# Two-layer vision block on one core: image 0's convolution chain inside the dense expert layer, gate logits from unnormalised rows, first expert tiles inside image 1's chain

## What is computed

```python
x = x + _L0_conv_ref(_ln_c(x), ...)
t = _to_tokens(x)
t = t + _L0_ffn_ref(_ln_t(t), ...)          # 8 experts, all computed
x = _from_tokens(t, x)
x = x + _L1_conv_ref(_ln_c(x), ...)
t = _to_tokens(x)
t = t + _L1_ffn_ref(_ln_t(t), ...)          # 16 experts, top 2 of a softmax

def _L1_conv_ref(x, ...):
    h = _group_norm(1x1 conv to 32 channels)
    z = relu(_group_norm(9-tap column conv + 9x9 depthwise conv of h))
    z = relu(_group_norm(1x1 conv to 128 channels))
    return z + x

def _L1_ffn_ref(x, ...):
    probs = softmax(x @ gate_w + gate_b); two largest, scaled to sum 1
    hidden = silu(x @ w1[e]) * (x @ w2[e])
    return sum over the two e of gate * (hidden @ w3[e])
```

## Time and profile before

| | us |
|---|---|
| median of 3 runs (721.44 to 726.18) | 723.17 |
| the profiled execution | 719.29 |
| its span, first to last instruction | 717.5 |
| busy: TensorE, GpSimd, VectorE, ScalarE | 599.5, 424.2, 358.2, 356.0 |
| mean granted TensorE clock, share of full | 0.902 |

### The profile page before, as it was taken

One profiled execution on the slowest core, in us unless ns is written; L12 is line 12 of the kernel. 1 busy time (PEld: TensorE's weight loads), 2 busy tenths in 40 slices (PEclk: granted clock), 3 DMA queues, 4 the chain that ended last, 5 costly groups with the idle time before them and its releaser, 6 DMA issues.

```text
span 717.5 us, 16640 instructions
## 1 busy us (share of the span) xinstructions
PE 599.5 (84%) x5672; PEld 506.2 (71%) x5673; DVE 358.2 (50%) x1040; ACT 356.0 (50%) x843; POOL 424.2 (59%) x484
## 2 busy tenths in 40 slices
PE   2677788879699999999999989887869999999900
PEld 2566677667377776677777667676869999999900
DVE  6977788655600612030014554573755555555533
ACT  4466678975564445751135532224036665666600
POOL 1667799764785686663342200077567777777771
PEclk9989999988888899999997998886879999999965
DMA  9452222211256353231490000011223332333536
GB/s 308 142 139 79 80 69 83 58 52 50 86 201 221 115 201 132 90 132 45 138 320 18 1 0 1 0 49 53 64 58 99 109 97 83 109 99 93 199 117 212
DMA packets 59042, 75.35 MB, mean 105 GB/s; under 512 B 9470, under 2 KB 49366, under 8 KB 58302
## 3 DMA queue, kind: packets, MB, share of 16 engines
q1 hardware_dynamic: 51614, 60.49, 26.7%
q0 software_dynamic: 5632, 11.62, 4.8%
q10 hardware_dynamic: 1728, 2.36, 0.9%
HBM read 57.96 MB, written 23.81 MB: 114 GB/s over the span
## 4 chain that ended last, share of the span: by engine, by line
PE 62%; DVE 10%; POOL 10%; issue 7%; ACT 7%; DMA 3%; SPq 1%; DVEq 0%; POOLq 0%; ACTq 0%
PE bank L800 13%; PE bank L762 9%; PE bank L866 8%; PE bank L745 8%; PE bank L811 6%; PE bank L831 4%; PE bank L722 3%; POOL gathered_or_att L570 3%; POOL padded_or_w L561 3%; PE bank L316 3%; POOL returned L640 2%; POOL gathered_or_att L579 2%; ACT normed L911 2%; PE bank L881 2%; PE bank L791 2%
## 5 line engine op out<-in xcount | busy, mean ns | idle before, releaser
L605 POOL TENSOR_TENSOR padded_or_w<-padded_or_w,gathered_or_att 128x384 f32<-128x384 f32 x96 | 95.3, 999 | 76.9 <-ACT padded_or_w L985 73.1
L621 POOL DMA_INDIRECT sorted_x<-normed,slot x72 | 71.7, 995 | 97.0 <-DVE slot L1328 75.8
L640 POOL DMA_INDIRECT returned<-gathered_or_att,home_of_slot x104 | 102.7, 987 | 31.7 <-issue 22.3
L985 ACT ACTIVATE padded_or_w<-bank,moe_b 128x384 f32<-128x384 f32 x96 | 55.4, 580 | 102.9 <-PE bank L745 102.8
L762 PEld LDWEIGHTS bank<-moe_or_conv,padded_or_w 128*128 128x128 f32 x576 | 82.3, 201 | 32.0 <-issue 10.9
L762 PE MATMUL bank<-moe_or_conv,padded_or_w 128*128 128x128 f32 x576 | 85.6, 288 | 0.0
L745 PE MATMUL bank<-chan_major,moe_or_conv 128*128 128x384 f32 x192 | 83.0, 520 | 0.0
L660 PE MATMUL bank<-padded_or_w 64*64 64x64 f32 x1152 | 49.3, 239 | 26.7 <-issue 15.3
L660 PEld LDWEIGHTS bank<-padded_or_w 64*64 64x64 f32 x1152 | 43.2, 150 | 36.4 <-issue 36.4
L1357 DVE TENSOR_TENSOR att_or_moe<-att_or_moe,bank 128x256 f32<-128x256 f32 x104 | 43.7, 420 | 50.3 <-PE bank L811 27.0
L999 ACT ACTIVATE att_or_moe<-bank 128x256 f32<-128x256 f32 x104 | 40.0, 384 | 55.9 <-PE bank L800 55.9
(11 more groups left out here) (181 smaller groups left out, 1166.8 us busy)
## 6 DMA issues: line engine op xcount, KB each, us to landing
gathered_or_att<-combine SPq DMA_DIRECT2D x24, 768.0 KB, 4.1
padded_or_w<-windows SPq DMA_DIRECT2D x192, 48.0 KB, 1.9
...
```

The source lines that it names most:

```text
L605: nc.gpsimd.tensor_tensor(HB[n % DRING], HB[n % DRING], GB_[k % 3][:, n % 4, :], ALU.mult).then_inc(S("gated"), 1)
L621: nc.gpsimd.indirect_dma_start(xs_dram[b], bass.IndirectOffsetOnAxis(ap=POS[b][:, k, t:t + 1], axis=0), TNR[b][:, t, :], None).then_inc(S( ...
L640: nc.gpsimd.indirect_dma_start(yt_dram[b], bass.IndirectOffsetOnAxis(ap=HOMES[b][:, j:j + 1], axis=0), YR[k * RING + j % RING], None).then ...
L985: nc.scalar.activation(HB[n % DRING], banks[HBANK[n % 2]][:, 0:DG], ACT.Gelu, bias=B1C[:, e:e + 1]).then_inc(S("gelu"), 1)
```

## The change

Image 0's whole chain up to its slots and its scatter stands in the dense layer, closer packed: the taps six groups per step, the eight up-projections, the relu, the sum, the routing. The list behind the dense layer holds image 1's chain alone, with 20 of the 160 `KW` matmuls. The gate logits no longer wait for the last norm: the gate weights are centred once (`GC`), 18 matmuls take the rows of the first norm (`LB`, in two halves), 18 the convolution's output (`LZ`, three per group beside `XZ`), and VectorE adds both and scales by 1/std. So `RT` and `LG` of layer 1 are gone, and the normalised rows are needed by the scatter alone; ScalarE makes all of them. Square roots of three of the norms and of image 1's last two group norms become Newton steps on VectorE, those of image 0's group norms a power on GpSimd (`PG`). The table of tile experts is a phase of its own (`RJ`). The first 14 pipeline steps of image 0's tile loop (`MT`) stand between phases of image 1's chain, on all engines; the loop uses other PSUM banks, a tile's transpose and output share one, and ScalarE evicts the output before the silu.

```diff
...
+            (33, ("RX", 1)), (40, ("GC", 0)), *every(28, 4, groups("AN", "LR", 0, 1))])
...
-            (52, ("SQ", "XL", 0)), (52, ("LV", "XL", 0)), *every(53, 1, groups("LT", "XL", 0)), *every(54, 1, groups("XG", 0)),
-            *every(56, 2, groups("AN", "XL", 0)), (61, ("XC", 0)), (62, ("XCE", 0)), (62, ("GN", "XC", 0)), (65, ("GS", "XC", 0)), (67, ("GQ", "XC", 0)),
-            (69, ("XCH", 0)), *every(71, 1, taps(0, 0, 54)), (89, ("GN", "XM", 0)), (91, ("GS", "XM", 0)), (93, ("GQ", "XM", 0)), (95, ("XMH", 0)),
-            *every(96, 1, [("XU", 0, n) for n in range(4)])])
-        order += [("KW", 24, "gelu", DN), *normed("XL", 1), *[("XU", 0, n) for n in range(4, 8)], ("GN", "XU", 0), *groups("XG", 1), ("GS", "XU", 0), ("GQ", "XU", 0),
-                  ("XC", 1), ("XCE", 1), ("GN", "XC", 1), ("KW", 10, "hc_ready", 2 * NB), ("GS", "XC", 1), ("GQ", "XC", 1), ("XCH", 1), ("KW", 12, "hc_ready", 2 * NB), *groups("XUH", 0),
-                  *taps(1, 0, 9), *groups("XZ", 0), *groups("AN", "XL", 1), *taps(1, 9, 24), *routing(1, 0), *taps(1, 24, 54),
-                  *choice(1, 0, 1, 6), ("GN", "XM", 1), ("KW", 6, "hc_ready", 2 * NB), ("GS", "XM", 1), ("RP", 0), ("GQ", "XM", 1), ("XMH", 1), ("RS", 0),
-                  *[("XU", 1, n) for n in range(8)], ("GN", "XU", 1), ("KW", 30, "up_out", 8 * NB), ("GS", "XU", 1), ("GQ", "XU", 1), ("KW", 10, "up_out", 8 * NB), *groups("XUH", 1), *groups("XZ", 1),
-                  ("KW", 18, "up_out", 8 * NB), *routing(1, 1), ("KW", 34, "up_out", 8 * NB), *choice(1, 1, 1, 6), ("RP", 1), ("KW", 16, "up_out", 8 * NB), ("RS", 1),
-                  *[("M", b) for b in range(NB)], *[("F", b) for b in range(NB)]]
-
-        group_no = {ph: k for k, ph in enumerate(ph for ph in order if ph[0] in ("LNA", "YA", "RT", "LG", "RX", "XG", "XZ"))}
+            (52, ("LV", "XL", 0)), *every(52, .5, groups("LT", "XL", 0)), *every(53, .5, groups("XG", 0)),
+            *every(56, 2, groups("AN", "XL", 0)), (57, ("XC", 0)), (58, ("XCE", 0)), (58, ("GN", "XC", 0)), (59, ("LB", 0, 0)), (60, ("GS", "XC", 0)),
+            (61, ("LB", 0, 1)), (61, ("PG", "XC", 0)), (63, ("XCH", 0)), *every(64, 1 / 6, taps(0, 0, 54)), (66, ("GN", "XM", 0)), (68, ("GS", "XM", 0)),
+            (69, ("PG", "XM", 0)), (71, ("XMH", 0)), *every(72, 1 / 3, [("XU", 0, n) for n in range(8)]), (74, ("GN", "XU", 0)), (77, ("GS", "XU", 0)),
+            (78, ("PG", "XU", 0)), *every(79, .5, groups("XUH", 0)), *every(80, .25, [(kind, 0, g) for g in range(NG) for kind in ("XZ", "LZ")]),
+            (85, ("LN", "LR", 1, 0)), (85, ("LV", "LR", 1, 0)), (86, ("RC", 1, 0, 0)), (88, ("RE", 1, 0)), (89, ("RC", 1, 0, 1)), (90, ("RC", 1, 0, 2)),
+            (92, ("RC", 1, 0, 3)), *every(91, 2, groups("LT", "LR", 1, 0)[:2]), (94, ("RC", 1, 0, 4)), (95, ("RP", 0)), (96, ("PD", 1)), (96, ("RS", 0)),
+            *every(96, .5, groups("LT", "LR", 1, 0)[2:])])
+        order += [*normed("XL", 1), *groups("XG", 1), ("XC", 1), ("XCE", 1), ("GN", "XC", 1), ("LB", 1, 0), ("GS", "XC", 1), ("GQ", "XC", 1), ("XCH", 1),
+                  ("LB", 1, 1), *groups("AN", "XL", 1), ("RJ", 0), *taps(1, 0, 54),
+                  ("GN", "XM", 1), ("KW", 8, "hc_ready", 2 * NB), ("GS", "XM", 1), ("KW", 12, "hc_ready", 2 * NB), ("XMH", 1), *[("XU", 1, n) for n in range(8)],
+                  ("GN", "XU", 1), ("GS", "XU", 1), *tiles(0, 4), *groups("XUH", 1), *[(kind, 1, g) for g in range(NG) for kind in ("XZ", "LZ")],
+                  ("LN", "LR", 1, 1), *tiles(4, 6), ("LV", "LR", 1, 1), ("RC", 1, 1, 0), ("RE", 1, 1), *groups("LT", "LR", 1, 1), *tiles(6, 7), ("RC", 1, 1, 1),
+                  *tiles(7, 9), ("RC", 1, 1, 2), *tiles(9, 11), ("RC", 1, 1, 3), *tiles(11, 13), ("RC", 1, 1, 4), ("RP", 1), *tiles(13, 14), ("RS", 1), ("RJ", 1),
+                  *tiles(14, J + 4), ("M", 1), *[("F", b) for b in range(NB)]]
...
-            return ln[0] in ("LNA", "LR", "XL") and not (g % 2 == 0 and tuple(ln) in (("LNA", 0), ("LNA", 1), ("XL", 1), ("LR", 1, 0), ("LR", 1, 1)))
+            return ln[0] in ("LNA", "LR", "XL") and not (g % 2 == 0 and tuple(ln) in (("LNA", 0), ("LNA", 1), ("XL", 0), ("XL", 1)))
...
+        NEWTON = (("XL", 0), ("LR", 1, 0), ("LR", 1, 1))
...
-        UP = ((6, 7), (4, 5, 3, 2))
+        UP = ((6, 7), (4, 5))
...
+        HID_BANK, ROW_BANK = (6, 7), (2, 3)
...
+                    sp.wait_ge(S("y_used"), DN)
...
+                nc.gpsimd.tensor_tensor(gv[:, 9:10], gv[:, 5:6], EXPO[:, 0:1], ALU.pow).then_inc(S("gn_root"), 1)
...
+                ln_wait_all(pool, "LR", 1, b)
...
+            def norm_logits(b, h):
+                E, n = EX[1], group_no[("LB", b, 0)]
+                if h == 0:
+                    t_wait_read(pe, group_no[("GC", 0)])
+                    t_wait_all_read(pe, "XG", b)
+                    t_wait_bank(pe, n)
+                for t in range(h * TT // 2, (h + 1) * TT // 2):
+                    ins = nc.tensor.matmul(t_bank(n)[:, t * E:(t + 1) * E], QY[b][:, t * P:(t + 1) * P], GWC[:, :], start=True, stop=True)
+                if h:
+                    ins.then_inc(S("t_full"), 1)
+
+            def conv_logits(b, g):
+                E = EX[1]
+                pe.wait_ge(S("z3_ready"), b * NG + g + 1)
+                for t in range(g * TG, (g + 1) * TG):
+                    ins = nc.tensor.matmul(banks[LOGIT_BANK[b]][:, t * E:(t + 1) * E], QY[b][:, t * P:(t + 1) * P], GWC[:, :], start=True, stop=True)
+                if g == NG - 1:
+                    ins.then_inc(S("conv_logits"), 1)
...
-                    nc.tensor.transpose(banks[r % 2][:, 0:P], XS[h * RING + r], IDN).then_inc(S("x_transposed"), 1)
+                    if not isinstance(j, int) or j >= 6:
+                        pe.wait_ge(S("y_ready"), j - 5 + b * J)
+                    elif b and j < 2:
...
-                    if isinstance(j, int) and j == 0 and b == 0:
-                        pe.wait_ge(S("routed1"), 1)
                     pe.wait_ge(S("hid1"), j + 1 + b * J)
-                    if not isinstance(j, int) or b or j >= 2:
+                    if isinstance(j, int) and j + 4 >= J:
                         pe.wait_ge(S("y_ready"), j - 1 + b * J)
...
+                    if j >= 4:
+                        act.wait_ge(S("y_full1"), j - 3 + b * J)
...
                     if j < J:
                         xt(j, j % RING)
+                    if j >= 4:
+                        tail(j - 4, j % RING)
                     if 0 <= j - 2 < J:
                         nonlin(j - 2, (j - 2) % RING)
-                    if j >= 4:
-                        tail(j - 4, j % RING)
...
                 lv = ln_set(ph)
-                dve.wait_ge(S("ln_std"), lns.index(ph) + 1)
-                link(nc.vector.reciprocal(lv[:, 5, :], lv[:, 4, :]))
+                if ph in NEWTON:
+                    chain_done = lns.index(ph) + 1
+                    dve.wait_ge(S("ln_var"), chain_done)
+                    newton(lv[:, 3, :], lv[:, 5, :], lv[:, 4, :])
+                    link(ts(lv[:, 5, :], lv[:, 5, :], NEWTON_SCALE, None, ALU.mult))
+                else:
+                    dve.wait_ge(S("ln_std"), [ln for ln in lns if ln not in NEWTON].index(ph) + 1)
+                    link(nc.vector.reciprocal(lv[:, 5, :], lv[:, 4, :]))
                 nc.vector.scalar_tensor_tensor(lv[:, 6, :], lv[:, 0, :], -1.0, lv[:, 5, :], ALU.mult, ALU.mult).then_inc(S("ln_coef"), 1)
...
                 row, v, over_e, over_t = route_views(l)
 
                 if piece == 0:
+                    if l == 1:
+                        dve.wait_ge(S("conv_logits"), b + 1)
+                        link(tt(RT[:, 0, 0:c], LGP[b][:, :], banks[LOGIT_BANK[b]][:, 0:c], ALU.add))
+                        link(tt(row(0), row(0), over_e(ln_set(("LR", 1, b))[:, 5, :]), ALU.mult))
+                        link(tt(row(0), row(0), over_t(GB[:, :]), ALU.add))
...
+            def norm_logits(b, h):
+                if h == 0:
+                    return
+                E, m = EX[1], group_no[("LB", b, 0)]
+                lv = ln_set(("XL", b))
+                link(tt(ONE_STD[:, :], lv[:, 3, :], lv[:, 5, :], ALU.mult))
+                link(ts(ONE_STD[:, :], ONE_STD[:, :], 1.0, None, ALU.add))
+                t_wait_full(dve, m)
+                t_read(tt(LGP[b][:, :].rearrange("p (t e) -> p t e", e=E), t_bank(m)[:, 0:TT * E].rearrange("p (t e) -> p t e", e=E),
+                          ONE_STD[:, :].unsqueeze(2).broadcast_to([P, TT, E]), ALU.mult), m)
...
+            def newton(v, y, t):
+
+                link(ts(y.bitcast(i32), v.bitcast(i32), 1, None, ALU.logical_shift_right))
+                link(ts(y.bitcast(i32), y.bitcast(i32), -1.0, float(0x5f3759df), ALU.mult, ALU.add))
+                for three in (3.0, 12.0, 768.0):
+                    if v.shape[-1] == 1:
+                        link(nc.vector.scalar_tensor_tensor(t, y, y, v, ALU.mult, ALU.mult))
+                    else:
+                        link(tt(t, y, y, ALU.mult))
```

(16 more changed lines are left out.)

170 lines of the change are left out of this document (112 added, 58 removed).

## The result

Over 15 runs of each the changed kernel took 730.22 us (median, 724.36 to 742.86), the kernel before 721.62 (715.18 to 726.18). The ratio is 1.0111, 95% interval 1.0073 to 1.0149: slower by one per cent, as forecast (732 us, 1.2 per cent over 723.17). The profiled execution took 726.65 us, its span is 724.8 where 726.5 was forecast; before it was 717.5.

A forecast was written before the change was run, and what follows sets the result against it. GpSimd's indirect DMA queue behind image 1's slots was taken as the bound: 543.5 + 0.3 + 168.5 + 14.2 = 726.5 us span, 732 us on the scale of the median. Its own range was 728 to 740, the overall range 718 to 742.

The forecast's parts named there:

- What bounds: GpSimd's indirect DMA queue sets the end: image 1's slots, then 0.3 us, 130 DMAs in 168.5 and a 14.2 us tail.
- Stage 1: Dense layer, paced by TensorE: 16.2 us added, 8.0 old idle off, 6.0 stalls and 4.3 clock added; end at 406.7.
- The add behind the slots: On VectorE image 0's slots, 7.1 us, stand ahead of the dense layer's last add, which starts at 411.0.
- Stage 2: Image 1 from its norm to its exponentials, in five parts: 93.9 us instead of 115.5, 21.6 us shorter.
- Stage 3: Image 1 from exponentials to slots: 36.8 us instead of 16.2, 20.6 more, slots at 543.5.
- silence: After image 1's exponentials VectorE does nothing for 10.2 us, its multiply waiting for a silu queued on ScalarE.
- The signs named for a right forecast: GpSimd unbroken over 130 DMAs, first scatter 538 to 549, norm 408 to 417, VectorE silent some 10 us, clock 0.50.
- A: Rival, faster: clock holds at full speed, 16.1 us less, span 710.4, time 716; chance 0.14.
- B: Rival, no change: packed dense layer regains its idle time, stage 1 7.3 us shorter, time 725; chance 0.26.
- C: Rival, much slower: the tile loop becomes the bound, over 1.67 us a tile; time 744 at 1.8; chance 0.06.
- D: Rival: group norms' square roots on GpSimd are dear, holding the dense layer 7.8 us, time 740; chance 0.05.
- The Trainium skill's drain: Rule for ScalarE table switches: a drain of 1.38 us each, 2.66 instead of 1.28 for stage 3's silu load.

The follow-up runs named there:

- e3: Changed kernel with image 0's slots moved on VectorE behind image 1's first norm; 1.0109 of the time of the kernel before.
- e2: Changed kernel with ScalarE's 18 normalisations of image 1's rows moved behind tile step 13, tiles left in place; 1.0154 of the kernel before.
- e1: Changed kernel with image 0's tile steps 4 to 13 moved behind image 1's slots; no ratio, 4 executions of 717.48 to 733.17 us.
- e4: Changed kernel with all of image 0's tile steps, 0 to 13, moved behind image 1's slots; 0.9958 of the kernel before.
- e7: Changed kernel, all tiles behind image 1's slots, image 0's slots behind image 1's norm, GpSimd's additions before image 0's scatter, idle-filling matmuls added; 0.9874 of the kernel before.
- e8: Changed kernel with image 0's first 36 logit passes cut from two runs of 18 into six runs of 6; 1.0183 of the kernel before.

## Why the prediction was right, and which terms were off

**What bounds.** Right, term by term: slots to scatter 0.76 us (0.3 forecast), 130 DMAs 168.2 (168.5), tail 14.9 (14.2). Slots at 540.96 instead of 543.5, and 534.5 was break-even. In every run the span followed the slot time and the number of DMAs behind it, with up to 3 us between executions in the pace of the DMAs.

**Stage 1.** Dense layer finished at 405.1, forecast 406.7, and this agreement is in part luck. The matmul with which the output of image 1's first group begins stands at 281.33 in the profile of before and at 278.01 in this one. In the eleven kernels made by the change, alike up to there, it stands between 277.94 and 281.66, so I put these 3.3 us down to the execution and not to the change.

```profile
281.33 0.91 PE L760 MATMUL bank<-moe_b,att_or_moe 24*128 24x384 f32 x2
```

```profile
278.01 0.91 PE L844 MATMUL bank<-moe_b,att_or_moe 24*128 24x384 f32 x2
...
357.91 0.75 PE L970 MATMUL bank<-conv_mid,conv_w 32*128 32x288 f32 x4
...
369.46 0.74 PE L805 MATMUL bank<-gate_w_centred,qy 128*128 128x16 f32 x6
```

From that matmul to the end of the layer TensorE took 106.9 us before and 127.1 here, 20.2 more, where the terms of the forecast add up to 18.5; from there to the end of the span the profile lost 10.6 us and not 7.3, and the ratio of all executions, 1.0111, lies between (8.0 us). The terms were further off than their sum. The added work was some 4 us cheaper than 16.2: from start to start the 72 narrow passes took 7.4 us (10.0 forecast), four up-projections 1.4 (2.8). The rows that they were priced from lie at the half clock, the 4.75 us in part (0.57 from 228 to 230; that row is of layer 0, with 8 columns), the 5.57 us almost wholly (0.59 from 460 to 462, then 0.50), so part of the clock was charged twice. TensorE idled 3.2 us at the first norm, 2.1 at the up-projections, 1.1 at the relu and 2.6 at the exponentials, 9.3 us with the small ones, where 6.0 were charged. Of these, 5.2 had been for the first norm and its gelu; the 3.2 at the up-projections and the relu had been put at nothing; and the table swap, taken at 0.8, had left out the 1.61 us in which ScalarE waits for VectorE between its loads. The clock fell three times instead of once:

```profile
298.00:304.00 6.00, 6.00 (x26) 4.30 (x26) 0.73 (x4) 1.06 (x2) 2.13 (x3) 0.72 0.35 131
346.00:352.00 6.00, 4.54 (x23) 2.89 (x22) 3.08 (x7) 3.51 (x7) 2.92 (x3) 0.94 0.35 131
352.00:358.00 6.00, 5.41 (x24) 3.54 (x22) 1.48 (x3) 2.55 (x5) 0.99 (x1) 0.78 0.00 0
394.00:400.00 6.00, 6.00 (x29) 3.93 (x29) 5.76 (x12) 3.48 (x9) 3.56 (x4) 0.86 1.01 277
```

These falls cost some 5 us, against 4.3 charged: 6 us times what is missing to 1.00 in the four rows is 4.2, and 1.0 for the 2 us ahead of the last one, from 391.94. What is left of the 20.2 us puts the old idle and half-speed time at about 6.3 us, where 8.0 were taken off. The add behind the slots was right to 0.05 us (4.3 forecast, 4.35 measured in e3).

**Stage 2.** 94.9 us against 93.9: to the first tap 17.9 (18.2), taps 28.7 (28.7), to the first up-projection 9.1 (6.2), to the relu 18.0 (17.0), to the exponentials 21.3 (23.8). The miss in the third part is the operation that GpSimd's additions held for 3.3 us. The prediction had costed GpSimd by its own length and its cover, and had not asked what it does to VectorE beside it. The last part was 2.5 us shorter than forecast, which hides most of that miss.

**Stage 3.** 34.7 against 36.8, in the parts forecast: silence 9.2 (10.2), the choice and slots alone 16.7 (16.2), tiles and restarts 8.8 (10.5). e2 shows the cause of the silence, e1 and e4 the whole price. The signs named for a right forecast came, the clock at 0.50 beside the narrow matmuls only in part: in the dense layer all 72 narrow passes ran at the full-speed pace, and in image 1's chain some did.

**The rivals.** A, the clock at full speed: it fell in the dense layer and in image 1's chain, as charged, and e7 shows what holding it at the six groups is worth: 3.2 us there, 1.9 in the chain. B, a packed layer that regains its idle time: 9.3 us idle and three falls, refuted. C: refuted by the fourth stretch; the loop's last matmul ended at 692.2 (690 forecast). D: the roots took 0.55 to 0.57 us on GpSimd and held nothing. The Trainium skill's drain (ScalarE: Activation LUTs, What ACT_TABLE_LOAD costs) did not show: behind the load that ended at 514.89 the silu started at 514.90. Its rule that idle gaps lower the clock (TensorE: Matmul & The Clock Gate, Why this matters for your kernels) agrees with e7, where filling the gap ahead of the six groups brought 0.50 to 1.00 under the same narrow matmuls. The fall during layer 0's 36 narrow passes, has no gap ahead of it in any of the twelve profiles, TensorE being busy from 206 on. Whether the fall behind the run of 18 does is open, as e8 leaves it.
